# A sparse-attention block kernel: index heads summed on TensorE, 36 blocks picked by 0/1 products, unread products in the last tile alone

## The reference, cut to what matters

```python
q_i = (x @ idx_wq).reshape(B_, L_, N_IDX_HEAD, D_HEAD)      # 4 heads of 64
k_i = x @ idx_wk
s_i = jax.nn.relu(jnp.einsum('bthd,bsd->bths', q_i, k_i))
I = jnp.einsum('bths,h->bts', s_i, idx_w)                   # sum over heads
I = jnp.where(local[None], jnp.inf, I)                      # the last 64 keys
I = jnp.where(causal[None], -jnp.inf, I)
_, idx = jax.lax.top_k(I, kk)                               # 96 keys
key_c = (c_kv @ W_uk)[bi, idx]...                           # keys and values of these
```

## Time and profile before

| what | us |
|---|---|
| three runs | 823.52, 830.40, 831.96 |
| median | 830.4 |
| the profiled execution's own time | 824.12 |
| its span (first to last instruction) | 822.3 |
| PE busy, of the span | 768.5 |
| DVE busy | 647.5 |
| ACT busy | 510.3 |
| POOL busy | 505.0 |

### The profile page before, as it was taken

The page is one execution under the profiler, slowest core; times in us unless marked ns, Lnnn a source line. Parts: engine busy times, 40 slices in busy tenths (PEclk is TensorE's granted clock), DMA queues, the critical chain, the costliest instruction groups (busy, mean ns, idle before and its releaser), DMA issues.

```text
span 822.3 us, 17288 instructions
## 1 busy us (share of the span) xinstructions
PE 768.5 (93%) x5708; PEld 459.9 (56%) x5709; DVE 647.5 (79%) x1906; ACT 510.3 (62%) x1464; POOL 505.0 (61%) x528
## 2 busy tenths in 40 slices
PE   8787899999999999999999999899999888999986
PEld 4334456565656565656565566566669334545554
DVE  4879798888999998979899999943232589696874
ACT  5556586675877888778887786686624243344331
POOL 6777777777777777777777776777710734212210
PEclk9898899999999999999999999999999999999998
DMA  8412211211111111111111111129136100000000
GB/s 276 93 26 54 53 35 43 51 36 40 31 28 31 26 30 30 28 31 27 30 31 28 29 30 25 32 69 246 45 113 187 45 7 1 0 14 2 13 1 26
DMA packets 58824, 39.97 MB, mean 49 GB/s; under 512 B 26960, under 2 KB 49712, under 8 KB 58544
## 3 DMA queue, kind: packets, MB, share of 16 engines
q1 hardware_dynamic: 41568, 21.57, 10.2%
q0 software_dynamic: 14336, 15.72, 8.4%
q10 hardware_dynamic: 2832, 1.58, 0.7%
HBM read 33.31 MB, written 5.55 MB: 47 GB/s over the span
## 4 chain that ended last, share of the span: by engine, by line
PE 62%; DVE 15%; ACT 9%; issue 8%; POOL 3%; DMA 2%; DVEq 0%; ACTq 0%; SPq 0%; POOLq 0%
PE psI L663 7%; PE psK L647 6%; PE psP L828 4%; ACT R L928 4%; PE psK L766 3%; PE psS L1771 3%; PE psS L802 3%; PE psP L835 3%; PE psK L754 3%; PE psP L817 3%; PE psS L805 3%; PE psP L647 2%; PE psS L845 2%; POOL R L1556 2%; DVE SC L1144 2%
## 5 line engine op out<-in xcount | busy, mean ns | idle before, releaser
L630 POOL DMA_INDIRECT G<-key_rows,idx x320 | 320.7, 1002 | 101.7 <-issue 95.7
L663 PE MATMUL psI<-kiT,qiT 64*128 64x512 f32 (+5 forms) x320 | 85.7, 559 | 13.6 <-ACT R L928 12.3
L647 PE MATMUL psK<-cst 128*128 128x512 bf16 x339 | 93.6, 383 | 1.3 <-ACT KT L1034 1.3
L1058 ACT ACTIVATE PT<-psP 128x256 f32<-128x256 f32 x128 | 48.4, 378 | 70.0 <-PE psP L835 66.3
L1144 DVE SCALAR_TENSOR_TENSOR SC<-R,w_x,SC 128x512 f32<-128x512 f32 (+5 forms) x120 | 78.4, 653 | 11.6 <-ACT R L928 8.6
L1172 DVE MAX8 top<-SC 128x8 f32<-128x128 f32 (+15 forms) x64 | 78.4, 1225 | 2.4
L1174 DVE FIND_INDEX8 idxf<-top,SC 128x8 uint32<-128x128 f32 (+15 forms) x64 | 78.2, 1222 | 0.0
L928 ACT ACTIVATE R<-psI 128x512 f32<-128x512 f32 (+5 forms) x160 | 73.3, 510 | 6.3 <-PE psI L663 4.8
L1026 ACT ACTIVATE PR<-PR,rinv 128x208 f32<-128x208 f32 x128 | 58.5, 457 | 26.0 <-DVE rinv L1335 24.4
L1034 ACT ACTIVATE KT<-psK 96x512 f32<-96x512 f32 x108 | 63.8, 591 | 15.7 <-PE psK L754 14.7
L1327 DVE CUSTOM_DVE_ANT_0 S<-psS,cst 128x208 f32<-128x208 f32 x128 | 46.9, 367 | 21.7 <-PE psS L805 21.7
(11 more groups left out here) (361 smaller groups left out, 1723.0 us busy)
## 6 DMA issues: line engine op xcount, KB each, us to landing
G<-key_rows,idx POOLq DMA_INDIRECT x320, 2.4
rtmp<-idx_rows SPq DMA_DIRECT2D x20, 128.0 KB
xslots<-zrow SPq DMA_DIRECT2D x4, 320.0 KB, 11.0
SC<-xslots SPq DMA_DIRECT2D x8, 160.0 KB
yslots<-SC ACTq DMA_DIRECT2D x8, 160.0 KB, 2.5
V<-val_rows SPq DMA_DIRECT2D x15, 80.0 KB
xr<-in_x SPq DMA_DIRECT2D x1, 1024.0 KB, 11.5
qiT<-in_w_gate SPq DMA_DIRECT2D x4, 256.0 KB, 4.4
```

The lines of the kernel that those rows point to most:

```text
L630: pool.indirect_dma_start(ring[o % RING][:, g % GPB, DR:], None, key_rows, bass.IndirectOffsetOnAxis(ap=idx[:, t, g:g + 1], axis=0),).then ...
L647: pe.matmul(ps[:, :].rearrange("p (a n) -> p a n", a=2), warm_w, warm_x, start=True, stop=True, skip_group_check=True)
L663: pe.matmul(psI[i][:, 0:w], lhs, kiT[64 * i:64 * i + 64, CH * c:CH * c + w], start=True, stop=True).then_inc(s["i_mm"], 1)
```

## The change

Three things are changed together.

1. The index heads are summed on PE. `index_pair` is laid out anew: for each group of 32 queries the four heads lie one below the other in the rows of one bank, eight small products (64 rows by 32 columns) for a pair instead of two of 64 by 128. After ACT's four positive parts, `head_sum` multiplies each group with a small matrix of the weights (four products of 128 rows by 32 columns into the bank psX), and ACT copies the sum to SC (`sum_copy`). `combine` on DVE is gone.
2. HOT has 36 blocks: 4 to 39, which is all of tiles 0 to 4 but the first four blocks of tile 0. So POOL gathers 88 blocks, 40 to 127. `KTM` is 5 instead of 4.
3. The unread products of `front` and `p_transpose` stay only in tile 15; `WARM_TAIL` is as before.

With it come a new `index_plan` (the scans of tiles 1 to 5 are pulled ahead: `START_ROOM` 2.2, `LEAD` 5, `LEAD_LEVEL` 3.2), and a move of the router's small outputs from the bank psX to the last quarter of psP, with copies on ACT (`logits_copy`, `counts_copy`) and waits on PE (`beside_free`, `values_out`) that go with it.

```diff
-HOT = (4, 5, 6, 7, 8, 9, 10, 11, 16, 17, 18, 19, 24, 25, 26, 27, 32, 33, 34, 35)
+HOT = (4, 5, 6, 7, 8, 9, 10, 11, 12, 13, 14, 15, 16, 17, 18, 19, 20, 21, 22, 23, 24, 25, 26, 27, 28, 29, 30, 31, 32, 33, 34, 35, 36, 37, 38, 39)
...
-WARM_FIRST, WARM_GAP, WARM_TILE, WARM_K, WARM_P, WARM_T = 9, 2, 10, 2, 1, 0
+WARM_FIRST, WARM_GAP, WARM_K, WARM_P, WARM_TILES = 9, 2, 2, 1, 1
...
+KTM = max(key_tiles(m) for m in HOT)
...
-START_ROOM = 1.1
+START_ROOM, LEAD, LEAD_LEVEL, SPREAD = 2.2, 5, 3.2, (4, 9)
+OTHER = (0.0, 0.9, 1.9, 1.3, 0.0, 0.6, 0.0, 0.8)
...
+    def budget(n, level):
+        if n < 0:
+            return START_ROOM
+        return max(0.0, level - (0.7 if n >= 3 else 0.0) - OTHER[n % NB] - (0.25 * key_tiles(n) + 0.2 if n in HOT else 0.0))
...
+            for k in range(TOP_STEPS):
+                ready = done_at[chunk_base(t + 1) - 1]
+                while left <= 0 or n < ready:
+                    n += 1
+                    left = min(left, 0.0) + budget(n, LEAD_LEVEL if t <= LEAD else level)
...
-        PX = psX[:, 0:P]
+        PX = psP[:, 3 * P:4 * P]
...
                     for i in range(2):
-                        lhs = qiT[64 * i:64 * i + 64, pair, P * t:P * (t + 1)]
-                        pe.matmul(psI[i][:, 0:w], lhs, kiT[64 * i:64 * i + 64, CH * c:CH * c + w],
-                                  start=True, stop=True).then_inc(s["i_mm"], 1)
+                        for h in range(NIH):
+                            rows, at = slice(64 * (h % 2), 64 * (h % 2) + 64), QPG * (h ^ i)
+                            lhs = qiT[rows, h // 2, P * t + QPG * (2 * pair + i):P * t + QPG * (2 * pair + i + 1)]
+                            mm = pe.matmul(psI[i][at:at + QPG, 0:w], lhs, kiT[rows, CH * c:CH * c + w],
+                                           start=True, stop=True, skip_group_check=True)
+                        mm.then_inc(s["i_mm"], 1)
+
+                def head_sum(t, c):
+
+                    w = min(CH, keys_of(t) - CH * c)
+                    m = chunk_base(t) + c
+                    if m == 0:
+                        pe.wait_ge(s["w_cp"], 2)
+                    else:
+                        pe.wait_ge(s["i_first"], m)
+                    pe.wait_ge(s["i_relu"], 4 * (m + 1))
+                    for g in range(P // QPG):
+                        mm = pe.matmul(psX[QPG * g:QPG * (g + 1), 0:w], w_sum[:, g % 2, :], R[:, m % 2, g, 0:w],
+                                       start=True, stop=True, skip_group_check=True)
+                    mm.then_inc(s["comb"], 1)
...
-                    keep_warm(psK, WARM_TILE if b == 2 else WARM_K)
+                    if t >= NT - WARM_TILES:
+                        keep_warm(psK, WARM_K)
...
                     if n not in HOT:
-                        keep_warm(psP, WARM_P if n + LAG_T < NT * NB else WARM_T)
+                        if n >= NB * (NT - WARM_TILES) and n + LAG_T < NT * NB:
+                            keep_warm_beside(WARM_P)
...
+                    if n + 1 in index_sums:
+                        head_sum(*index_sums[n + 1])
+                    if n in index_pairs:
+                        index_pair(*index_pairs[n])
...
+                def sum_copy(t, c):
+
+                    w = min(CH, keys_of(t) - CH * c)
+                    act.wait_ge(s["comb"], chunk_base(t) + c + 1)
+                    if c == 0 and t >= 2:
+                        act.wait_ge(s["topk"], TOP_STEPS * (t - 1))
+                    act.activation(SC[:, t % 2, CH * c:CH * c + w], psX[:, 0:w], ACT.Copy).then_inc(s["i_first"], 1)
...
-                def combine(t, c):
-
-                    w = min(CH, keys_of(t) - CH * c)
-                    m = chunk_base(t) + c
-                    dst = SC[:, t % 2, CH * c:CH * c + w]
-                    dve.wait_ge(s["i_first"], m + 1)
-                    dve.wait_ge(s["i_relu"], 4 * (m + 1))
-                    for h in range(1, NIH):
-                        if h > 1:
-                            dve.wait_ge(s["comb"], 3 * m + h - 1)
-                        dve.scalar_tensor_tensor(out=dst, in0=R[:, m % 2, h, 0:w], scalar=w_i[:, h:h + 1], in1=dst,
-                                                 op0=ALU.mult, op1=ALU.add).then_inc(s["comb"], 1)
```

More of the change, by code:

```diff
@@ L38 @@
 NIH = 4
+QPG = 32
 KTS, LW = 96, 64
@@ L161, in cost @@
         return (1.04 * keys_of(t) / 1000 + 0.07) if i < TOP_STEPS - 1 else 0.1
-    other = (0.0, 0.9, 1.9, 1.3, 0.0, 0.6, 0.0, 0.8)
-    def hot(n):
-        return 0.25 * key_tiles(n) + 0.2 if n in HOT else 0.0
     def lay(level):
[L169 to L190, removed]
+        plan, done_at, top_end, n, left = {}, {m: N0 for m in range(chunk_base(3))}, {}, N0 + 1, 0.0
@@ new lines, in lay @@
+        for t in range(1, NT):
+            if t + 1 < NT and t + 1 >= 3:
+                for c in range(chunks_of(t + 1)):
+                    m = chunk_base(t + 1) + c
+                    at = n + (c + 1) * SPREAD[t > LEAD] // (chunks_of(t + 1) + 1)
+                    done_at[m] = max(at, done_at[m - 1] + 2, N0 + 4, top_end.get(t - 1, N0) + 2 if c == 0 else N0)
+            for k in range(TOP_STEPS):
[3 more added lines that the diff above has]
+                    left = min(left, 0.0) + budget(n, LEAD_LEVEL if t <= LEAD else level)
+                plan.setdefault(n, []).append((t, k))
+                left -= cost(t, k)
+            top_end[t] = n
@@ L196, in index_plan @@
     plan, done_at, _ = lay(level)
-    pairs = {}
+    pairs, sums = {}, {}
     for t in range(3, NT):
         for c in range(chunks_of(t)):
-            m = chunk_base(t) + c
[L202 to L209, removed]
+            at = done_at[chunk_base(t) + c]
+            sums[at] = (t, c)
+            for u in range(2):
+                pairs[at - 4 + u] = (t, 2 * c + u)
+    return pairs, sums, plan
 C_ID = 0
@@ L648, in keep_warm, with keep_warm_beside @@
                                   skip_group_check=True)
+                def keep_warm_beside(count):
+                    for _ in range(count):
+                        pe.matmul(psP[:, 0:3 * P].rearrange("p (a n) -> p a n", a=2), warm_w, warm_beside, start=True,
+                                  stop=True, skip_group_check=True)
                 def index_pair(t, u):
@@ L946, in _ @@
                 act.preload_act_table_set("natural_log_exp_and_others")
+                act.wait_ge(s["ld_w"], 16)
+                for i in range(2):
+                    act.activation(w_sum[:, i, :], w_rows, ACT.Copy, scale=w_i[:, i:i + 1]).then_inc(s["w_cp"], 1)
                 def projected(c, parts):
@@ L963, in _ @@
                     relu_pair(1, u)
+                sum_copy(1, 0)
                 for h in range(2):
@@ L2243 @@
             spread[3 * E1, col] = 1.0
+    idx_weights = np.stack([np.repeat(a("L0_attn_idx_w").reshape(NIH)[[h ^ i for h in range(NIH)]], QPG)
+                            for i in range(2)], 1)
     arrays = {
```

139 lines of the change are left out of this document (79 added, 60 removed).

## The result

The changed kernel takes 870.57 us (median of four runs, 866.96 to 877.78); beside it the kernel before took 826.96. The ratio is 1.0538, with a 95% interval of 1.0434 to 1.0643. The direction was forecast, the size wasn't: 870.6 lies above the range of 817 to 866. Some executions of a kernel are disturbed, over 1.5% above its fastest: ratios here leave them out, and where the profiled execution was one (those of a_warm3 and a_few), it is read for the order of its events and its granted clock alone.

What follows compares the result with a forecast made beforehand. It took POOL's gathers, restarting on block 40's values, to bound the stage: +30 us slip less 7.5 slack (22), less 4 for quicker gathers, +18, gave 842 for the profiled execution; predicted 845 us, range 817 to 866.

Steps and rivals of the forecast that it cites:

- the model of the stage: Blocks 68 to 127: POOL restarts when block 40 has given its values, and its gathers then take 314.5 us.
- catches up with POOL late: Steps 48 to 127: PE, with 80 steps in about 285 us, catches up, so POOL's last gather ends the stage.
- the slack of 7.5 us: At block 68: block 40's values came at 256.9, the gather started at 264.4, so 7.5 us of slip was free.
- the 4 us of quicker gathers: Gathers from block 68 on: without combine beside them, 4 us off the 314.5, between 0 and 6.
- a step behind 48 at less than 4.0 us: PE in steps 48 to 127: some 4.2 us loses 0.67 of unread products and gets 0.4 of head sums.
- inside the range: Waits on PE before the head sum: at most an ACT copy, given no term of their own.
- (a) Before block 0: Scans of tiles 1 to 5 pulled ahead and some eleven more pairs: +14 us, between 9 and 20.
- (b) to (d), steps 0 to 47: Changes to block 40's time: steps 0 to 7 -2 us, steps 8 to 39 +25, steps 40 to 47 -7.
- Picking by 0.68 us a key tile: Sixteen more picked blocks, 56 key tiles at 0.68 us each on PE: 38.1 us up to step 47.
- The rival of serial products: New pairs on PE need two rounds, 49 us more up to step 47, time near 890; chance 0.08 with the clock's fall.
- The clock rival: Behind step 100 PE's clock falls, PE ends some 45 us beyond POOL, about 890; chance 0.08 shared with serial products.
- the slip of block 40: Block 40's values, step 47, come +30 us later than in the kernel before, within 17 to 36.

Runs made afterwards that it cites:

- a_warm3: The kernel after with the unread products put back in the last three tiles (13 to 15) instead of the last alone; 873.6 us, ratio 1.0557.
- a_few: The kernel after with only the first of each block's four gathers issued from block 68 on (wrong outputs); 865.1 us in the one run left.
- b_few: The kernel before with three of four gathers of every block from 68 on left out; 827.4 us, ratio 1.0019.
- a_hot20: The kernel after with the 20 picked blocks of the kernel before instead of 36; 850.7 us, ratio 1.0281.
- a_warm16: The kernel after with unread products ahead of gathered blocks' fronts and probabilities' transposes in all tiles; 872.7 us, ratio 1.0562.
- The room runs: The kernel after, unread products in all tiles, START_ROOM 2.2 against 0.6: ratios 1.0562 and 1.0362 with 36 picked blocks, 1.0266 and 1.0024 with 20.
- b_hot36: The kernel before with the 36 picked blocks of the kernel after, nothing else changed; 859.2 us, ratio 1.0423.

## Why the prediction was wrong

**The step that failed** is the model of the stage: that its end is block 40's values plus 314.5 us of gathers, because PE, with its 80 steps behind step 47 in some 285 us, "catches up with POOL late, and POOL ends the stage". These 80 steps, from block 40's values to block 120's, took PE 328.5 us (323.2 before). POOL waits and restarts as forecast, at block 68 and for block 40, 34.3 us later for a slip of 41.3; but the stage follows PE. b_few shows it for the kernel before, a_few, with one run, and the chain that passes by the gathers for the kernel after. A stream without a gap was read as a bound; it was one whose loss costs 1 us. Two terms of the sum were there for POOL and worth nothing for the end: the slack of 7.5 us, and the 4 us of quicker gathers (from block 68 on POOL was busy with them for 234.2 instead of 239.9 us, but then stood 8.9 for the indices of the last tiles). Together they are 11.5 us. In a_hot20 and a_warm16, where PE came early enough, the last gathers do end the stage as the model says (in a_warm16 only from the last tile's indices on); after isn't one of them.

**On balance PE regains nothing.** I put a step behind 48 at less than 4.0 us. The steps from 49 to 97 lie in the first of these stretches of before and of after (columns as in the earlier trace rows):

```profile
267.00:472.00 205.00, 199.78 (x1726) 121.12 (x1725) 188.21 (x487) 163.06 (x499) 157.36 (x157) 1.00 0.13 29
```

```profile
311.00:516.00 205.00, 187.21 (x2068) 105.46 (x2065) 158.24 (x428) 160.99 (x512) 155.93 (x162) 0.97 0.16 30
546.00:606.00 60.00, 59.94 (x376) 39.95 (x368) 30.27 (x98) 34.64 (x116) 40.16 (x43) 0.50 0.28 64
```

Both need 205 us, 4.28 for each of 48 steps. Groups of before's unread products there, and of after's PE work (us busy, mean ns, then the idle time ahead and what ended it):

```profile
L647 PE MATMUL psK<-cst 128*128 128x512 bf16 x144 | 39.4, 383 | 0.0
...
L647 PE MATMUL psP<-cst 128*128 128x512 bf16 x48 | 18.4, 383 | 0.0
```

```profile
L656 PE MATMUL psI<-kiT,qiT 64*32 64x512 f32 (+4 forms) x528 | 34.0, 572 | 8.5 <-ACT R L963 8.4
...
L670 PE MATMUL psX<-R,w_sum 128*32 128x512 f32 (+4 forms) x144 | 18.2, 579 | 0.0
...
L888 PE MATMUL psP<-w_router,x1T 128*128 128x32 f32 x12 | 2.3, 272 | 2.8 <-ACT ot_region L1109 2.8
L896 PE MATMUL psP<-onehot,cst 128*128 128x32 f32 x12 | 2.3, 272 | 2.2 <-ACT ot_region L1109 2.2
```

By the earlier trace rows the products held up PE for 144 x 0.22 + 48 x 0.23 = 42.7 us. In their place stand 18 head sums of 1.00 us (below) = 18 us, 17.8 instead of 5.2 us of idle PE (+12.6), which is pairs waiting for ACT's positive parts and the moved router steps waiting for ACT to copy the output (queued ahead of the next scores now), and a clock of 0.97. I had priced the head sums and left the waits at "inside the range". Behind that the slip rises and falls. PE's timeline in before and in after, values of blocks 90, 100 and 112:

```profile
470.38 0.42 PE L835 MATMUL psP<-PT,G 128*32 128x32 f32 x8
...
509.69 0.42 PE L835 MATMUL psP<-PT,w_first 128*32 128x32 f32 x8
...
553.03 0.42 PE L835 MATMUL psP<-PT,G 128*32 128x32 f32 x8
```

```profile
513.90 0.42 PE L860 MATMUL psP<-PT,w_first 128*32 128x32 f32 x8
...
544.68 0.42 PE L860 MATMUL psP<-PT,G 128*32 128x32 f32 x8
...
599.52 0.64 PE L860 MATMUL psP<-PT,G 128*32 128x32 f32 x8
```

It is 43.5 us at block 90, 35.0 at block 100 and 46.5 at block 112: at full clock PE did regain 8.5 us, and in 546 to 606, busy for 59.94 of 60 us at half clock, it lost 11.5. How the 42.7 us split to the last us, and what the stage would take at full clock without unread products, or with the clock held and fewer gathers, no run here shows. What is shown is that neither returning the clock alone (a_warm16) nor, with one run, taking the gathers away alone (a_few) brings the time down.

**(a) Before block 0** is the term of the sum that was most mis-sized: +22.6 us instead of +14, beyond my 9 to 20. DVE's and PE's groups of the kernel after from 20 to 80 us:

```profile
L1200 DVE TENSOR_TENSOR SC<-SC,cst 128x128 f32<-128x128 f32 x5 | 1.5, 299 | 11.2 <-ACT SC L972 11.1
```

```profile
L656 PE MATMUL psI<-kiT,qiT 64*32 64x512 f32 (+4 forms) x288 | 16.7, 521 | 11.6 <-ACT R L963 11.6
```

I counted the scans' busy time, and it is there; but each index now comes by PE, ACT, PE and ACT to DVE, and DVE stands for 11.1 us until the copied sums arrive. The room runs confirm the place: 2.2 to 0.6 gives back 2.0 to 2.4% (12 to 14 us by the times themselves).

**(b) to (d), steps 0 to 47**, forecast +16 (-2, +25, -7): measured 41.3 - 22.6 = +18.7. Picking by 0.68 us a key tile was right: with the unread products that go with these 16 blocks it is 38.1 - 1.6 - 10.7 = 25.8 us by the prediction's prices, and b_hot36, which has no other change, delays block 40 by 22.8.

**Head sums and pairs** run side by side as priced. PE's timeline in the kernel after, a head sum before block 0 (four products, each in two records), and a pair behind block 40:

```profile
53.50 1.06 PE L670 MATMUL psX<-R,w_sum 128*32 128x512 f32 x8
54.50 0.52 PE L656 MATMUL psI<-kiT,qiT 64*32 64x192 f32 x11
...
338.36 1.09 PE L656 MATMUL psI<-kiT,qiT 64*32 64x512 f32 x16
339.38 1.12 PE L740 MATMUL psM<-w_q,cq_region 64*128 64x512 f32 x2
```

The next product starts 1.00 us after the head sum's start and 1.02 after the pair's (expected 1.06 for both). The rival of serial products is out.

**The clock rival** was right in place (behind step 100) and wrong in size: it had PE end some 45 us beyond POOL. The stretch at half clock took back 11.5 us in after. As a way to win them the unread products are no use, since a_warm16 with them takes the same time.

**The sum again.** Forecast 842 for the profiled execution, whose span would be 840.2. Block 40 came 11.3 us later than I had it (41.3 for 30), slack and quicker gathers count for nothing at an end that PE sets (11.5), and the last values slip 6.3 us more than block 40: 840.2 + 29.1 = 869.3 of 870.5. That the forecast had the right sign owes to the slip of block 40, which it had in its parts, and too small.

## What to carry to other kernels

A queue that runs without a gap and ends together with the stage may only be keeping pace: take most of its work away in a throwaway kernel before an argument is built on it. That answer holds for that kernel alone: of two chains that end close together, a variant that speeds up one hands the end to the other. Compare the same step in both kernels all along a stage, since equal slips at its first and last step can hide a rise and a fall. Where an in-order engine sets the end, work removed from another engine buys nothing. When work is moved onto the packed engine, count the waits that it brings along (here for ACT), not its busy time alone.

## What the runs showed of the hardware

That PE can be busy for 59.94 of 60 us with the granted clock at 0.50 all the time, the level of 1.2 GHz, was new to me. The fall began behind a rest of PE of 1.74 us and the clock returned with the last tile's unread products:

```profile
544.10 0.41 PE L842 MATMUL psP<-cst,PR 128*128 128x128 f32 x2 [1.74 <-ACT ot_region L1109]
```

The Trainium skill's page "TensorE: Matmul & The Clock Gate", section "What's actually happening", says that the default state is throttled and that activity releases it. By the rows, 60 us of products that a profile counts as busy did not release it here, and with unread products among them (a_warm16) it was 1.00 in about the same steps.
